# Moving the next batch's key and value stages to other steps of the attention loop

## The reference

```python
# cross attention: 16 heads of 16, keys and values from the context, a mask over keys
q, k, v = heads(layernorm(x) @ wq.T), heads(ctx @ wk.T), heads(ctx @ wv.T)
x = x + softmax(where(mask, -1e9, q @ k.T / 4)) @ v @ wo.T
# then: of layernorm(x) the 128 rows with the highest score y @ w_router are chosen, and only
# they go through a small causal self-attention and a gated feed-forward block
y = layernorm(x)
x_sel = y[top_k(y @ w_router, 128)]
x_sel += causal_attention(rmsnorm(x_sel, g1)) @ W_out.T
x_sel += (silu(rmsnorm(x_sel, g2) @ W1.T) * (rmsnorm(x_sel, g2) @ W2.T)) @ W3.T
out = x + y.at[chosen].set(x_sel)
```

## Time and profile before

| | |
|---|---|
| median of 3 runs | 877.21 us (876.47 to 877.97) |
| the profiled execution | 877.64 us |
| its span | 875.8 us |
| TensorE busy | 844.8 us, 96% |
| ScalarE busy | 563.7 us, 64% |
| VectorE busy | 327.6 us, 37% |
| GpSimd busy | 123.3 us, 14% |

### The profile page before, as it was taken

One profiled execution on the slowest core, in us unless ns is written; L12 is line 12 of the kernel. 1 busy time (PEld: TensorE's weight loads), 2 busy tenths in 40 slices (PEclk: granted clock), 3 DMA queues, 4 the chain that ended last, 5 costly groups with the idle time before them and its releaser, 6 DMA issues. The chain is left out here.

```text
span 875.8 us, 27999 instructions
## 1 busy us (share of the span) xinstructions
PE 844.8 (96%) x11618; PEld 288.9 (33%) x11618; DVE 327.6 (37%) x945; ACT 563.7 (64%) x634; POOL 123.3 (14%) x174
## 2 busy tenths in 40 slices
PE   7999999999999999999999999999999999999875
PEld 2322222324323332334323333234323342234333
DVE  3132254323443345423543234522454223322452
ACT  3577657676677767677577766677666766877310
POOL 3100112021020111101111110201111111200111
PEclk9999999999999999999999999999999999999999
DMA  6080230111301220201301202012202100010000
GB/s 187 5 292 4 67 85 9 56 41 41 80 14 51 80 69 16 58 26 57 80 15 49 79 18 65 14 51 80 55 5 59 32 2 7 16 48 3 8 25 11
DMA packets 37706, 42.91 MB, mean 49 GB/s; under 512 B 3251, under 2 KB 32478, under 8 KB 37576
## 3 DMA queue, kind: packets, MB, share of 16 engines
q1 hardware_dynamic: 35080, 39.08, 15.1%
q0 software_dynamic: 2496, 1.98, 1.2%
HBM read 31.20 MB, written 12.60 MB: 50 GB/s over the span
## 5 line engine op out<-in xcount | busy, mean ns | idle before, releaser
L561 ACT ACTIVATE probs<-pair_bank 128x1024 f32<-128x1024 f32 x512 | 496.3, 1021 | 228.4 <-ACTq L560 226.4
L531 PE MATMUL pair_bank<-q_sb,k_sb 32*64 32x512 f32 x4096 | 293.9, 612 | 0.9 <-PEq L529 0.9
L550 PE MATMUL o_bank<-probs,va 128*32 128x512 f32 x2048 | 273.2, 604 | 2.7 <-PEq L547 1.2
L531 PEld LDWEIGHTS pair_bank<-q_sb,k_sb 32*64 32x64 f32 x4096 | 64.6, 129 | 145.3 <-issue 143.1
L550 PEld LDWEIGHTS o_bank<-probs,va 128*32 128x32 f32 x2048 | 41.7, 108 | 206.8 <-issue 114.6
L304 PE MATMUL m_bank<-wv_sb,ctx_in 128*32 128x256 f32 x1024 | 62.5, 380 | 2.7 <-PEq L319 2.7
L304 PE MATMUL m_bank<-ctx_in,wk_sb 128*32 128x512 f32 x480 | 61.0, 592 | 0.0
L701 DVE TENSOR_SCALAR va<-m_bank,valid 128x256 f32<-128x256 f32 x64 | 28.1, 479 | 81.9 <-DVEq L698 81.6
L642 DVE STREAM_TRANSPOSE o_blk<-o_bank 128x512 f32<-128x512 f32 x32 | 22.9, 717 | 76.7 <-DVEq L641 76.7
L304 PEld LDWEIGHTS m_bank<-wv_sb,ctx_in 128*32 128x32 f32 x1024 | 33.8, 110 | 39.5 <-issue 25.5
L1000 POOL DMA_INDIRECT in_order<-y_tok,place x28 | 29.2, 1042 | 101.9 <-POOLq L999 84.3
(11 more groups left out here) (177 smaller groups left out, 593.7 us busy)
## 6 DMA issues: line engine op xcount, KB each, us to landing
ctx_in<-in_ctxT SPq DMA_DIRECT2D x7, 1024.0 KB, 5.0
x<-in_x SPq DMA_DIRECT2D x8, 512.0 KB, 4.7
mask_in<-in_mask SPq DMA_DIRECT2D x8, 512.0 KB, 3.9
out_dram<-base SPq DMA_DIRECT2D x8, 512.0 KB, 5.4
x_in<-in_x SPq DMA_DIRECT2D x28, 128.0 KB, 4.2
turned<-blocks_t SPq DMA_DIRECT2D x28, 128.0 KB, 3.2
xn_t<-turned SPq DMA_DIRECT2D x7, 512.0 KB, 3.9
ctx_in<-in_ctxT SPq DMA_DIRECT2D x2, 512.0 KB, 7.6
```

Source lines behind the costliest of these rows:

```text
L531: last = nc.tensor.matmul(pair_bank[pairs[r // 2]][j:j + 64, r % 2], key_tile(b, s, r)[:, j:j + 64], query_tile(b, s, r), start=True, stop ...
L550: last = nc.tensor.matmul(o_bank[32 * r:32 * r + 32], va[b % 2][:, t, HV * h:HV * h + 32], probs[s % 2][:, r], start=(t == 0), stop=(t == ...
L561: nc.scalar.activation(probs[s % 2][:, 2 * e:2 * e + 2, :], pair_bank[p][:], ACT.Exp, scale=HD ** -0.5).then_inc(s_free[p], 1)
```

## The change

It changes the three tables of the loop for batches 1 to 7 and nothing else. TensorE: `K01` in two halves goes from steps 18 and 19 to 7 and 8, which had no stage. `V3`, whole in step 21, goes in two halves to 18 and 19. `K10` goes from 23 to 21. Step 23 has no stage. ScalarE: the copy of `K01` goes from 19 to 8, that of `K10` from 23 to 21, and `differ` from 21 to 23. VectorE: `V3` stands before `pv` and no longer behind it.

```diff
 PE_SLOT = [("P", "K00:1", 0, False), ("F", "wo0", 1, False), ("F", "wo1", 2, False), ("P", "V0", 3, True),
-           ("P", "K11:0", 4, False), ("P", "K11:1", 5, False), ("F", "spread", 6, False),
+           ("P", "K11:0", 4, False), ("P", "K11:1", 5, False), ("F", "spread", 6, False), ("P", "K01:0", 7, False), ("P", "K01:1", 8, False),
            ("P", "R0:0", 9, False), ("P", "R0:1", 10, False), ("P", "V1", 11, False), ("P", "R1:0", 12, False), ("P", "R1:1", 13, False),
            ("F", "hidT", 14, False), ("F", "q", 15, False), ("F", "k", 16, False), ("F", "v", FS_STEP, False),
-           ("F", "fs", FS_STEP, False), ("P", "V2", FS_STEP, False), ("P", "K01:0", 18, False), ("P", "K01:1", 19, False),
-           ("F", "pv", 20, False), ("P", "V3", 21, False), ("F", "wout", 22, False), ("P", "K10", 23, False), ("F", "hid2T", 24, False),
+           ("F", "fs", FS_STEP, False), ("P", "V2", FS_STEP, False), ("P", "V3:0", 18, False), ("P", "V3:1", 19, False),
+           ("F", "pv", 20, False), ("P", "K10", 21, False), ("F", "wout", 22, False), ("F", "hid2T", 24, False),
            ("F", "u0", 25, False), ("F", "w0", 26, False), ("F", "u1", 27, False), ("F", "w1", 28, False),
            ("F", "down:0", 29, False), ("F", "down:1", 30, False), ("X", "K00:0", 31, False)]
-ACT_SLOT = [("P", "K00", 0), ("P", "K11", 5), ("F", "spread", 6), ("F", "hidT", 14),
-            ("F", "v", FS_STEP), ("F", "fs", FS_STEP), ("P", "K01", 19), ("P", "differ", 21), ("P", "K10", 23), ("F", "hid2T", 24),
+ACT_SLOT = [("P", "K00", 0), ("P", "K11", 5), ("F", "spread", 6), ("P", "K01", 8), ("F", "hidT", 14),
+            ("F", "v", FS_STEP), ("F", "fs", FS_STEP), ("P", "K10", 21), ("P", "differ", 23), ("F", "hid2T", 24),
             ("F", "u0", 25), ("F", "u1", 27)]
 DVE_ORDER = [...
-             ("F", "base"), ("F", "q"), ("N", "norm1a"), ("F", "k"), ("N", "norm1b"), ("P", "V2"), ("F", "pv"), ("P", "V3"), ("F", "wout"),
+             ("F", "base"), ("F", "q"), ("N", "norm1a"), ("F", "k"), ("N", "norm1b"), ("P", "V2"), ("P", "V3"), ("F", "pv"), ("F", "wout"),
              ...
```

## The result

The changed kernel takes 885.99 us, median of four runs (883.5 to 890.91), against 877.29 for the kernel before in as many runs beside them: ratio 1.0108 (1.0084 to 1.0132). The ratios here are those on record, each with its 95% interval; the two medians alone would give 1.0099. It is slower, as forecast, but by 8.7 us and not 3.7, and the time lies above the range. The profiled execution took 885.11 with a span of 883.3, 7.5 more than before, and what follows explains these 7.5.

A forecast was written before the change was run, and what follows sets the result against it. TensorE, busy for 96% of the span, was taken to bound the kernel. Per batch 1.10 lost less 0.48 gained is +0.62, in six batches +3.7 us, so 877.21 becomes 880.9; 8-in-10 range 878.0 to 883.7.

The forecast's parts named there:

- ScalarE's lag: Steps 23 to 25: empty step 23 costs 0.34, late Exps behind `differ` 0.76; loss 1.10 us a batch, absorbed by step 25.
- (a): Rival, chance 0.10: late Exps cost only what batch 0 shows, 0.61 us; +0.13 in a batch, 878.0 us.
- (b): Rival, chance 0.15: TensorE pays for all of `differ`, 1.56 us; +1.08 in a batch, 883.7 us.
- (c): Rival, chance 0.05: the lag of ScalarE never reaches TensorE; the gain alone gives -2.9 us, 874.3 us.
- step 11: Behind the filled steps 7 and 8, `R0`, `V1` and `hidT` come 1.2 us later; nobody waits, nothing counted.
- steps 8 and 9: Filling steps 7 and 8 ends waits of 0.35 and 0.13 us in 8 and 9: gain 0.48 in a batch.
- L907: VectorE, behind `u0`, inside GpSimd's subtraction: keeps its 0.56 us, so `w0` waits for nothing; taken as zero.
- L900's row: VectorE line taking 0.84 us beside GpSimd's subtraction, 0.48 without; applied to L907, the total would be 0.8 us more.
- (d): Rival, chance 0.04: even, 877.2 us; stages in 7 and 8 relieve an unseen wait in steps 10 to 17, worth 0.62.
- The other queues: SyncE has the mask, then the context load behind it; context is read over 20 us later, in step 31: nothing.
- if steps 26 to 28 carry a wait too: Sign in batches 1 to 6 of the changed trace that the prediction is wrong; no size given.

The follow-up runs named there:

- e3: The kernel before with only `differ` moved from step 21 to 23: 881.67 us, ratio 1.0051 to the kernel before.
- e2: The changed kernel with `differ` back in step 21, ahead of the copy of `K10`: 874.53 us, ratio 0.9965 to the kernel before.
- e4: The changed kernel with `differ` in step 19: 874.82 us, ratio 0.9968 to the kernel before.
- e1: The changed kernel with SyncE's context load ahead of the mask loads: 881.67 us against 877.07 for the kernel before, ratio 1.0045.
- e6: e4 with the residual loaded behind the context instead of ahead of the store: 873.06 us, ratio 1.0005 to the kernel before.
- e11: The changed kernel with `differ` in 19, `K10` in 23, 21 empty, `wout` ahead of the values in 22, residual loaded behind the context: 875.1 us, ratio 0.9974.
- e8: The changed kernel again without edit, on the second chip: 887.01 us against 872.5 for the kernel before, ratio 1.0178.
- e9: e3 with the context load ahead of the mask, as in e1: 882.84 us against 877.04 for the kernel before, ratio 1.0073.

## Why the prediction was right and wrong

**Right: ScalarE's lag.** Each link came as worked out: 0.34 for the empty step, then `differ` between the Exps, the lag absorbed by step 25. 2.75 to 2.76 and 4.10 to 4.11 stand against 2.75 and 4.1, six times. e3 agrees from the other side: with step 23 at 3.76 instead of 2.04 the lag costs 0.25, and the values start 2.19 behind the late Exps, as in the prediction (batch 4, 503.72 and 501.53). e2 and e4 take the lag away with `differ` alone. Rivals (a) and (b) fall: the lag costs more than in batch 0 and less than all of `differ`. (c) falls, since the lag does reach TensorE. e2 and e4 come out near its 874.3, but by other terms, step 11 above all.

**Right: steps 8 and 9.** 0.47 in a batch (2.8 us in six), as taken.

**Right: L907.** Timelines of VectorE and GpSimd after, batch 6:

```profile
716.29 0.56 DVE L907 SCALAR_TENSOR_TENSOR silu<-half_tanh,m_bank 128x384 f32<-128x384 f32 x1 [3.61 <-DVEq L906]
```

```profile
715.09 2.79 POOL L972 TENSOR_TENSOR mask_in<-mask_in,mask_row 128x256 int32<-128x256 int32 x4 [6.34 <-POOLq L969]
```

L907 lies within the subtraction and keeps its 0.56, as do all its cases (553 to 555 ns). In the changed kernel it lies so only in this batch; in e1 and e3 it does in all six, and takes 553 to 555 ns there too. L900's row would have misled. The Trainium skill's rule ("SBUF — State Buffer", Who interferes with whom), that a VectorE instruction with at most one operand in SBUF does not contend with GpSimd, agrees with these rows.

**Wrong by 3.5 us: step 11.** The prediction said of the later `R0` and `V1` "so nobody waits for them", and dismissed rival (d) because "nothing that those steps need is made sooner". Both look at one side only. The need came later, and that frees a step from a wait just as well. The row was there to read: step 11 at 4.56 where a whole stage takes 3.77, and `m_bank`'s 0.61 before `V1`. I had summed the waits behind `probs` and compared only steps 7 to 9 and 18 to 25 with their nominal lengths. With this term the six batches come to 6.6 - 2.8 - 3.5 = +0.3: what four of them show, and what (d) had as its time.

**Wrong by 7.2 us: "The other queues ... Nothing."** This is the step that decided. I asked when the data of mask and context are needed, found 20 us to spare, and stopped. The data do have that time. What did not is TensorE's own instructions, which come by the same DMA engines. e1 takes the stop away by the order of loads alone, e3 makes it in TensorE's program of before, and e6 and e11 take nearly all of the one at step 17 away by moving another load. The counts above show that the packet is not late because TensorE gets to its block late: the packet's request itself has no row, but TensorE is at the same place at the same time, and the packet starts when the data are through. The prediction named its own sign of this, "if steps 26 to 28 carry a wait too", but gave no price for it and had no rival with it.

So the right sign was in part luck: the price that it stood on, the lag less steps 8 and 9, is cancelled by step 11, and what makes the kernel slower is what was put at nothing. By the other terms the change would be level, not slower, where the wait in step 11 exists and no instruction comes late.

**Open.** The four runs of the changed kernel reach from 883.5 to 890.91 and e8's five from 883.14 to 890.38, where those of before stay within 1.5 us in four runs and within 5.5 in the 31 beside e1 to e4. Only one execution of each run is traced, and the traces show stops that vary: step 12 of batch 0 also crosses a block, is edited in no kernel, and takes from 2.90 to 4.33. VectorE's silence behind L730 has no cause yet. All traces but those of before and e2 also have 3.4 us at half the clock in the tail, between 827 and 849. The median of e1 lies 0.4 us and that of e3 1.2 us further above before than their traces do.

## What to carry to other kernels

Before an edit is priced, list every step whose length is above its work, over the whole loop, and ask of each what a later need does to it, as well as an earlier supply. When a buffer's release moves, work out at what moment the loads behind it leave and what they leave with; loads that are not urgent can still hold back an engine's instructions, so keep bulk loads apart. If an engine stands with "issue" as its releaser, count its instructions: stops that lie whole blocks of 256 apart are late instructions. Side work of an in-order engine belongs behind its longest step, not in the empty one: here the place of `differ` alone parts 885.99 us from 874.53.

## What the runs showed of the hardware

A TensorE with 24,209 instructions in 880 us lives on one 16 KB packet about every 9 us. At step 26 of batch 1 the packet for a block came 1.0 us after TensorE began the block before when no data were on the way, and 5.68 after when 1.58 MB were; it then stood for 2.36 us.

After stops of 2.36 and 2.08 us in step 26 (changed kernel, e8), and of 2.11 and 2.19 in step 1 (e1, e9), the granted clock fell from 2.4 to 1.2 GHz, for 3.4 us each time; after 1.32 (e3), 1.01 (step 1 of the kernel before) and 0.50 (e9, step 26) it did not. A stop of 2.36 us so cost 4.3.

The same kernel took 877.07 us on the first chip, 877.04 on the third and 872.5 on the second, where the wait of 0.6 to 0.8 us in step 11 is absent in every trace, which is 3.5 of the 4.6 us. A change that works on such a wait has another ratio there: 1.0178 against 1.0108 for this one, in part by this wait.
